# Second normalisation folded into centred weights, and a new hand-written order of jobs, in an attention and expert kernel on one core

## The reference, cut to what matters

```python
def layernorm(x):                       # no learned scale or shift
    return (x - mean(x)) / sqrt(var(x) + 1e-5)

n = layernorm(x)
Q, K, V, U = silu(n @ Wq), silu(n @ Wk), silu(n @ Wv), silu(n @ Wu)   # U is used as silu(U)
s = (Q @ K.T + bias[i - j]) / 4         # per head, causal, keys that are zero masked
x = x + (silu(s) @ V) * U

n = layernorm(x)
logits = n @ w_gate.T                   # 8 of them, the best two taken
g = softmax over the best two, else 0
x = x + sum_e g[e] * ((n @ w_in[e].T) @ w_out[e].T)
```

## Time and profile before

| | us |
|---|---|
| median of 3 runs | 286.77 |
| lowest, highest | 285.39, 286.88 |
| the profiled execution | 285.98 |
| its span, first to last instruction | 284.2 |
| PE busy in it | 263.2 |
| DVE busy | 230.0 |
| ACT busy | 225.0 |
| POOL busy | 146.6 |

### The profile page before, as it was taken

How to read it: one execution, slowest core, us unless ns; L and a number is a source line. 1 busy time by engine, 2 the same in 40 slices (tenths; PEclk the granted TensorE clock), 3 DMA queues, 4 the chain that set the end, 5 groups by cost and what they waited for, 6 DMA issues and landing times.

```text
span 284.2 us, 8464 instructions
## 1 busy us (share of the span) xinstructions
PE 263.2 (93%) x3146; PEld 124.3 (44%) x3146; DVE 230.0 (81%) x764; ACT 225.0 (79%) x434; POOL 146.6 (52%) x236
## 2 busy tenths in 40 slices
PE   7779799999999999999999998999987999999862
PEld 5435444355565434243354444433442544554420
DVE  6448453744689997989999986999999999896977
ACT  2667998998777899899998999897666977879600
POOL 6312235330104559645964494569765649548554
PEclk9979999999999999999999999999999999999998
DMA  4796216986950004991496027803890100100101
GB/s 115 172 305 194 75 17 193 208 180 211 235 131 22 2 2 133 236 190 21 147 229 164 3 78 231 175 6 79 221 232 26 35 4 3 37 2 2 38 3 37
DMA packets 27912, 31.24 MB, mean 110 GB/s; under 512 B 3032, under 2 KB 16856, under 8 KB 27872
## 3 DMA queue, kind: packets, MB, share of 16 engines
q1 hardware_dynamic: 24320, 28.28, 39.8%
...
...
## 4 chain that ended last, share of the span: by engine, by line
PE 69%; DVE 16%; ACT 4%; DMA 4%; issue 3%; SPq 1%; POOL 1%; DVEq 0%; ACTq 0%; POOLq 0%
PE jobp L648 23%; PE o_acc L639 20%; PE score L623 20%; DVE score L914 9%; DMA wout_s<-in_L_ffn_w_out 3%; PE jobp L677 2%; DVE ymix L1026 2%; ACT wts L784 2%; PE jobp L709 2%; ACT xn L797 1%; PE jobp L729 1%; DVE xs L1040 1%; DVE stats L953 1%; SPq L452 1%; PE o_acc L743 1%
## 5 line engine op out<-in xcount | busy, mean ns | idle before, releaser
L914 DVE TENSOR_TENSOR score<-score,bias_near 128x256 f32<-128x256 f32 (+3 forms) x288 | 113.2, 468 | 13.7 <-PE score L623 13.3
L782 ACT ACTIVATE wts<-score 128x512 f32<-128x512 f32 (+1 forms) x172 | 96.7, 592 | 20.5 <-DVE score L914 16.5
L565 POOL TENSOR_TENSOR ymix<-ymix 128x512 f32<-128x512 f32 (+2 forms) x90 | 74.6, 829 | 48.6 <-DVE ymix L1026 43.9
L784 ACT ACTIVATE wts<-score,far 128x512 f32<-128x512 f32 x120 | 73.8, 700 | 6.6 <-DVE score L914 5.3
L639 PE MATMUL o_acc<-wts,v_pad 128*32 128x512 f32 (+3 forms) x864 | 77.1, 458 | 0.7 <-ACT wts L782 0.7
L648 PE MATMUL jobp<-mm_e,xn2T 128*32 128x512 f32 x480 | 60.3, 593 | 0.3 <-ACT mm_e L854 0.3
L623 PE MATMUL score<-q_stack,k_stack 64*128 64x256 f32 (+3 forms) x336 | 47.9, 356 | 0.1
L1026 DVE TENSOR_TENSOR ymix<-jobp,gates 128x512 f32<-128x512 f32 x60 | 40.3, 685 | 6.4 <-PE jobp L648 5.9
L623 PEld LDWEIGHTS score<-q_stack,k_stack 64*128 64x128 f32 x336 | 30.4, 184 | 31.0 <-issue 28.5
L639 PEld LDWEIGHTS o_acc<-wts,v_pad 128*32 128x32 f32 x864 | 20.8, 108 | 29.8 <-issue 16.1
L623 PE MATMUL score<-xn2T,xs 32*128 32x512 f32 (+3 forms) x192 | 26.9, 520 | 0.7 <-ACT wts L782 0.7
...
## 6 DMA issues: line engine op xcount, KB each, us to landing
...
```

What stands on the lines that cost most here:

```text
L565: then_wait(pool.tensor_tensor(y[:, 0:n], y[:, 0:n], y[:, n:2 * n], ALU.add))
L782: act.activation(weights, score[bank][:, 0:n], ACT.Silu, scale=HD ** -0.5).then_inc(weighed[bank], 1)
L784: act.activation(weights, score[bank][:, 0:n], ACT.Silu, bias=far[:, h:h + 1], scale=HD ** -0.5)\
L914: ins = dve.tensor_tensor(score[bank][:, c + near:c + n], score[bank][:, c + near:c + n], bias, ALU.add)
```

## The change

The second normalisation is no longer computed as such. Its mean is taken out of the weights: a matrix `centre` (1 - 1/128 on the diagonal, -1/128 elsewhere) is multiplied into the expert matrices and into w_gate by a new job `CM`. Its rstd is multiplied into the gap and the gates of every unit, as before in the last one alone. So `norm2`, `xn2` and `centred` go, `T2` transposes `xs` itself after `SEL`, and POOL makes no shift for these. POOL's `scale` waits for the gates of the unit that used the same rstd before, and `best` waits for `scaled` in every unit.

In the last unit `T2` stands ahead of `SEL`: products with the identity lay the old rows out by features in its bank, and after the gate two more add `oT`. `BEFORE`, `BESIDE` and `AFTER` are new throughout. The diff is cut to its core:

```diff
 BEFORE = [
-    [("stats1", 0, 0), ("RB",), ("norm1", 0, 0), ("stats1", 0, 1), ("T1", 0, 0), ("Q", 0, 0), ("K", 0, 0),
-     ("norm1", 0, 1), ("V", 0, 0), ("MASK", 0, 0)],
+    [("stats1", 0, 0), ("RB",), ("T1", 0, 0), ("norm1", 0, 0), ("norm1", 0, 1), ("stats1", 0, 1), ("Q", 0, 0),
+     ("K", 0, 0), ("T1", 0, 1), ("V", 0, 0), ("K", 0, 1), ("Q", 0, 1), ("MASK", 0, 0), ("REL",)],
 ]
 BESIDE = [
-    [("T1", 0, 1), ("U", 0, 0), ("stats1", 1, 0), ("WT", 0)],
-    [("M", 0), ("stats1", 1, 1), ("WT", 1)],
-    [("Q", 0, 1), ("K", 0, 1), ("norm1", 1, 0), ("M", 1), ("V", 0, 1), ("T1", 1, 0), ("norm1", 1, 1)],
+    [("stats1", 1, 0), ("WT", 0)],
+    [("M", 0), ("WT", 1), ("stats1", 1, 1)],
+    [("CM", 2), ("U", 0, 0), ("norm1", 1, 0), ("M", 1), ("U", 0, 1), ("T1", 1, 0), ("norm1", 1, 1)],
...
+    [("CM", 1), ("MASK", 1, 1)],
...
+    [("FF", 0, 3, 1), ("LOG", 1), ("best", 1, 0), ("best", 1, 1), ("gates", 1)],
+    [("V", 2, 0), ("U", 1, 1), ("T2", 2), ("T1", 2, 1), ("FF", 0, 4, 0), ("tanh", 1), ("FF", 0, 4, 1)],
...
+    [("FF", 2, 7, 0), ("best", 6, 0), ("best", 6, 1), ("gates", 6)],
+    [("tanh", 6), ("FF", 2, 7, 1)],
...
-    [("FF", 3, 3, 1), ("T2", 7)],
-    [("LOG", 7), ("tanh", 7), ("best", 7, 0), ("best", 7, 1), ("gates", 7)],
+    [("FF", 3, 1, 1), ("FF", 3, 2, 0), ("best", 7, 0), ("LOG", 7)],
+    [("FF", 3, 2, 1), ("tanh", 7)],
+    [("FF", 3, 3, 0), ("best", 7, 1), ("FF", 3, 3, 1)],
+    [("gates", 7)],
     [("FF", 3, 4, 0), ("FF", 3, 4, 1)],
 ]
 AFTER = [
...
-    [("SEL", 8), ("stats2", 8), ("norm2", 8), ("FF", 3, 5, 0), ("T2", 8), ("LOG", 8), ("best", 8, 0),
-     ("best", 8, 1), ("gates", 8), ("FF", 3, 5, 1), ("FF", 3, 6, 0), ("FF", 3, 7, 0), ("FF", 3, 6, 1),
-     ("FF", 3, 7, 1), ("tanh", 8), ("MIX",)],
+    [("FF", 3, 5, 0)],
...
+    [("T2", 8), ("SEL", 8), ("stats2", 8), ("LOG", 8), ("best", 8, 0), ("best", 8, 1), ("gates", 8),
+     ("FF", 3, 5, 1), ("FF", 3, 6, 0), ("MIX",), ("FF", 3, 7, 0)],
...
+    [("tanh", 8), ("FF", 3, 6, 1), ("FF", 3, 7, 1)],
@@ POOL, scale @@
+                elif b > 0 and ln:
+                    pool.wait_ge(gates_ready, 1 + unit_before(args[0]))
...
-                if (args, ln) in [((LAST,), 1), ((0, 0), 0)]:
+                if ln or args == (0, 0):
                     pool.tensor_tensor(rstd[:, ln, ts], rstd[:, ln, ts], mhalf[:, ts], ALU.pow).then_inc(scaled, 1)
                     return
...
+            then_wait(pool.memset(centre[:], -1.0 / D))
+            pool.affine_select(out=centre[:], in_=centre[:], compare_op=ALU.not_equal, fill=1.0 - 1.0 / D, base=0,
+                               pattern=[[-1, P]], channel_multiplier=1).then_inc(centre_set, 1)
@@ PE, T1 and T2 @@
+                        if job == ("T2", LAST):
+                            ins = pe.matmul(bank[:, cols], xs[:, b, t], ident[:], start=k == 0, stop=False)
+                        else:
+                            ins = pe.transpose(bank[:, cols], xn1[:, t] if kind == "T1" else xs[:, b, t], ident[:])
+                    if job == ("T2", LAST):
+                        pe.wait_ge(gated, LAST + 1)
+                        for k, t in enumerate(tiles):
+                            ins = pe.matmul(bank[:, k * P:(k + 1) * P], ident[:], oT[:, t * P:(t + 1) * P], start=False, stop=k + 1 == len(tiles))
@@ PE, the new job; LOG now waits for ("CM", 2) and uses wg_c, the first FF waits for ("CM", 0) and ("CM", 1) @@
+                elif kind == "CM":
+                    k = args[0]
+                    pe.wait_ge(centre_set, 1)
+                    if k < 2:
+                        for e in range(k * E // 2, (k + 1) * E // 2):
+                            wait_drained(pe, ("M", e))
+                        ins = quarters(bank[:], centre[:], mm_e[:, k * E // 2:(k + 1) * E // 2].rearrange("p e d -> p (e d)"))
+                    else:
+                        pe.wait_ge(wg_in, 16)
+                        ins = quarters(bank[:, 0:E], centre[:], wg_s[:])
@@ ACT copies CM's bank back to mm_e, or to wg_c; its norm2 goes @@
@@ DVE, take_best and mix_gates, now in every unit; its norm2 of the last unit goes @@
+                    dve.wait_ge(scaled, SCALES.index(((u,), 1)) + 1)
+                    then_wait(ins)
+                    dve.tensor_tensor(gap[:, ts], gap[:, ts], rstd[:, 1, ts], ALU.mult).then_inc(top_ready, 1)
...
+                then_wait(dve.tensor_tensor(pick[:, 0, ts], pick[:, 0, ts], rstd[:, 1, ts].unsqueeze(2).to_broadcast([P, n, E]),
+                                            ALU.mult))
```

More of the change, by code:

```diff
@@ L106 @@
 SPLIT = {s: n for n, s in enumerate(SPLITS)}
-BANKED = ("RB", "T1", "Q", "K", "V", "U", "MASK", "SEL", "T2", "LOG", "FF", "WT", "M")
+BANKED = ("RB", "T1", "Q", "K", "V", "U", "MASK", "SEL", "T2", "LOG", "FF", "WT", "M", "CM")
 LAST = len(UNITS) - 1
 LAST_TILES = range(NT - 2, NT)
+T2_FIRST = LAST
 def all_near(group):
@@ L155 @@
-    [("K", 1, 1), ("T2", 0), ("split", 1, 1)],
-    [("WT", 4), ("M", 3)],
-    [("LOG", 0), ("best", 0, 0), ("V", 1, 0), ("M", 4)],
-    [("WT", 5), ("tanh", 0)],
-    [("M", 5), ("WT", 6)],
-    [("MASK", 1, 0), ("best", 0, 1)],
-    [("gates", 0)],
-    [("WT", 7)],
-    [("stats1", 2, 0), ("MASK", 1, 1), ("M", 6)],
-    [("M", 7), ("V", 1, 1), ("FF", 0, 0, 0), ("norm1", 2, 0), ("FF", 0, 0, 1), ("SEL", 1)],
-    [("FF", 0, 1, 0), ("T1", 2, 0)],
-    [("FF", 0, 1, 1), ("stats2", 1), ("U", 1, 1)],
@@ L191 @@
-    [("gates", 3), ("K", 3, 1), ("MASK", 3, 0)],
-    [("best", 4, 0), ("LOG", 4), ("FF", 1, 4, 0)],
-    [("FF", 1, 4, 1), ("best", 4, 1), ("FF", 1, 5, 0)],
-    [("FF", 1, 5, 1), ("split", 3, 1), ("tanh", 4)],
-    [("gates", 4), ("FF", 1, 6, 0)],
-    [("FF", 1, 6, 1), ("FF", 1, 7, 0)],
-    [("FF", 1, 7, 1)],
-    [("FF", 2, 0, 0)],
-    [("FF", 2, 0, 1), ("FF", 2, 1, 0)],
-    [("FF", 2, 1, 1), ("V", 3, 1)],
-    [("FF", 2, 2, 0), ("stats2", 5), ("SEL", 5)],
-    [("norm2", 5), ("FF", 2, 2, 1), ("FF", 2, 3, 0), ("MASK", 3, 1)],
@@ new lines @@
+    [("V", 2, 0), ("U", 1, 1), ("T2", 2), ("T1", 2, 1), ("FF", 0, 4, 0), ("tanh", 1), ("FF", 0, 4, 1)],
+    [("FF", 0, 5, 0), ("FF", 0, 5, 1), ("MASK", 2, 0)],
+    [("FF", 0, 6, 0), ("K", 2, 1)],
+    [("best", 2, 0), ("LOG", 2), ("stats1", 3, 0), ("V", 2, 1), ("Q", 2, 1), ("best", 2, 1), ("stats1", 3, 1)],
+    [("tanh", 2), ("FF", 0, 6, 1), ("MASK", 2, 1), ("split", 2, 1)],
+    [("U", 2, 0), ("norm1", 3, 0), ("gates", 2), ("FF", 0, 7, 0)],
+    [("FF", 0, 7, 1), ("FF", 1, 0, 0)],
+    [("FF", 1, 0, 1)],
@@ new lines @@
+    [("U", 2, 1)],
+    [("FF", 1, 1, 0), ("norm1", 3, 1), ("FF", 1, 1, 1)],
+    [("T1", 3, 0), ("T1", 3, 1)],
+    [("K", 3, 0)],
+    [("FF", 1, 2, 0), ("SEL", 3)],
+    [("FF", 1, 2, 1), ("T2", 3)],
+    [("stats2", 3), ("FF", 1, 3, 0), ("U", 3, 0)],
+    [("LOG", 3), ("FF", 1, 3, 1)],
+    [("best", 3, 0), ("Q", 3, 0), ("SEL", 4)],
+    [("tanh", 3), ("best", 3, 1), ("gates", 3), ("split", 3, 0), ("T2", 4)],
+    [("stats2", 4), ("V", 3, 0)],
+    [("K", 3, 1), ("LOG", 4)],
+    [("FF", 1, 4, 0), ("FF", 1, 4, 1)],
@@ new lines @@
+    [("FF", 1, 5, 0), ("best", 4, 0), ("Q", 3, 1), ("best", 4, 1), ("split", 3, 1)],
+    [("FF", 1, 5, 1), ("tanh", 4), ("FF", 1, 6, 0)],
+    [("gates", 4), ("FF", 1, 6, 1), ("MASK", 3, 0)],
+    [("FF", 1, 7, 0), ("FF", 1, 7, 1)],
+    [("FF", 2, 0, 0), ("MASK", 3, 1)],
+    [("FF", 2, 0, 1)],
+    [("FF", 2, 1, 0), ("V", 3, 1)],
+    [("FF", 2, 1, 1)],
+    [("FF", 2, 2, 0), ("FF", 2, 2, 1)],
+    [("SEL", 5), ("FF", 2, 3, 0), ("stats2", 5)],
+    [("T2", 5)],
+    [("best", 5, 0), ("tanh", 5), ("LOG", 5), ("U", 3, 1), ("best", 5, 1), ("gates", 5)],
[4 rows of a table added]
```

117 lines of the change are left out of this document (43 added, 74 removed), and 30 rows, old and new, of the table BESIDE.

## The result

The changed kernel takes 284.65 us (median of 20 runs, 283.42 to 286.87), the kernel before beside it 287.06 us (20 runs). The ratio is 0.9929, 95% interval 0.9912 to 0.9947: 0.7% or 2.0 us faster. The medians as printed differ by 2.4 us because the ratio leaves out three of the 20 runs before, at 290.7 us and more, which fell in a slower state. The change goes in the forecast direction, lies inside the forecast range, and is half of the 3.9 us. The profiled execution took 283.42 us, with a span of 281.5.

A forecast was written before the change was run, and what follows sets the result against it. TensorE leads with VectorE and ScalarE close behind, and 18 us of PE's steps are stalls. The terms from start to last unit sum to -3.9 us, from the 286.77 us median to 282.9 us; range 278.6 to 286.8.

The forecast's parts named there:

- Steps 8 to 17: These steps take 1.5 us more PE work into steps 13 to 16, which stalled 2.4 us: minus 0.7 us.
- Steps 18 to 35: Here 2.5 us more PE work and 2.2 us more on VectorE, 1 us absorbed: plus 1.5 us.
- Steps 36 to 48: Here 0.8 us less PE work, and the 1.0 us stall of step 41 partly gone: minus 1.2 us.
- Steps 49 to 63: PE has 7 us of stall, VectorE barely 1; VectorE's load sets the stretch, much as before: minus 1.0 us.
- The last unit: At the end, earlier gate and T2 waiting for it alone bring gap times rstd 1.5 us forward; minus 1.1 us counted here.
- The start: T1, K and Q of half 1 go ahead of the first scores, under PE's wait for wout: minus 1.0 us.
- The fourth rival: Longer pauses before 13 us put PE at half clock through the first work: 285.2 us, chance 0.08.
- Part 1: Normalisation leaves ScalarE in units 0 to 7: about 13 us net, little on the path; T2 needs only SEL's sum.
- Part 3: Centring products CM 0, 1 and 2 add 2.0 us on PE; CM 2's wait for w_gate taken as 0.
- VectorE waiting for tanh in order: Rival: gates of units 1 and 6 stand before their tanh, up to 7.2 us of waits, 290.1 us, chance 0.12.
- The halved stalls: Rival: freed ScalarE and short chain cut stalls from 18 us to 9: minus 8, 278.8 us, chance 0.20.
- VectorE's load as the bound of the middle: Rival: the middle's gains are eaten, only start and last unit stay: 285.6 us, chance 0.15.

The follow-up runs named there:

- e7: Changed kernel without the centring products CM 0 and CM 1 and their ScalarE copies, CM 2 kept: 0.9941 of the kernel before.
- e8: Changed kernel with the casts of split and the logits copies moved from VectorE to ScalarE, unit 5's tanh behind LOG and U: 1.0148 of before.
- e9: Changed kernel with 30 dummy 128-column activations put back on ScalarE after stats2 of units 0 to 7: 1.0236 of before, 293.86 us.
- e2: The changed kernel's algebra run through the old lists, norm2 left out and CM set in where its inputs are first made: 1.0117 of before.
- e1: Changed kernel without the two rstd products of units 0 to 7 on VectorE, the last unit keeping its own: 0.9893 of before.
- e3: Changed kernel with unit 5's tanh moved behind LOG and the copy of U: 0.9935 of before.
- e4: Changed kernel with the last unit's T2 behind SEL, two transposes of summed rows instead of four products: 0.9903 of before.
- e6: The kernel before with only the start of the lists from the changed one, CM left out: 1.0028 of before.
- e5: New algebra in the old lists, as e2, but with the CM products moved to other places: 1.0137 of before.

## Why the forecast was right in sign and half in size

- **Steps 8 to 17 (-0.7): -0.52.** Right, and for the reason given: e7 shows that CM's work lies in waits.
- **Steps 18 to 35 (+1.5): +2.18.** Undersized by 0.7 us. The step that failed is "1 us absorbed" of 2.5: 0.3 were. The stalls counted in these steps were taken as room for any engine's work, and work put in comes out at the end: e8 and e9 lengthen this stage too, by 2.87 and 3.03 us. Work taken out did not shorten it: in e2 ScalarE has 3.1 us less in it (54.46 us busy for 57.54), for 60.87 us and 60.78.
- **Steps 36 to 48 (-1.2): -1.69.** Right; step 41, with its stall, went from 4.75 to 2.37 us, partly because it has less work in it.
- **Steps 49 to 63 (-1.0): -0.12.** This is the largest miss, and the step of the forecast that failed: "with the norm chain gone, DVE's load sets it, much as before", and yet a gain of 1.0 was booked. VectorE was busy 49.53 us of 51.16 and is busy 49.28 of 51.04, so there was next to nothing to gain by the forecast's own rule. The chain of the earlier trace rows ended at 218.16 us as a wait of ScalarE; e2, which takes it away and adds the rstd products, has 51.15 us for 51.16. The products cost 0.61 us of the stage in the new lists (e1), and two drains of experts fewer (16 for 18, at 683 ns) stand against them. If the products cost as much in the old lists, the chain's end alone was worth about as much there; no run has the one without the other.
- **Steps 64 to 71 (-0.4): +0.04.** The 0.38 us of the last weights were read as a wait for ScalarE's tanh. The same was tried in another unit (e3) and was worth nothing. For this unit it is argued, not shown.
- **The last unit (-1.1): -1.40**, better by 0.3, though two of its reasons were off: the gate came 0.43 us earlier, not 0.7 (0.95 after the product's start for 1.38), and e4 shows the products in one bank to be worth nothing. Their price was right: two products behind the gate took 0.61 us for the forecast 0.6. The Trainium skill (TensorE: Matmul & The Clock Gate, Terms) has the transposing mode "4× faster for FP32"; taken as against a product, as the forecast took it, that makes an estimate of 1.2 us for the two. The trace does not agree: a transpose took 0.16 to 0.20 us (four in 0.63, two in 0.39) and a product 0.31.
- **The start (-1.0): not shown.** The medians leave 0 to 1.0 us for it, e6 has no gain from the new start in the old kernel, and the two profiles, which differ by 1.19 us at step 8, can't tell: they differ by 3.4 us for the same kernel code. The fourth rival, "a slow TensorE at the start", was written as a case that holds or not. It holds in some executions of this kernel and not in others: of the ten profiled executions with all of the new start, four kept the full clock from 16 to 28 us. CM 2 did not wait for w_gate; step 1 takes 7.38 us with it and 7.32 without (e6).

In sum from step 8 on: forecast -2.9, measured -1.51. **Part 1** said of the ScalarE time saved (13 us, 9.1 on the page) that "little of it is on the path by itself" and that what counts is the shorter way to T2. e2, which has both of these and pays for the rstd products, gains 0.2 us from step 18 to 63, so both together are worth little more there than the products cost. What was missing is that the new order spends what was freed: put 12.4 us back there, and 8.1 come out at the end (e9). **Part 3** had 2.0 us more on PE: in the old order 3.7 to 4.1 us (e5, e2), with whatever else the algebra moved there, in the new one 0 to 0.4 us for 1.7 (e7). So the algebra in the old lists costs 1.2%, and from there the lists give 1.9%. Nobody ran the new lists with the old normalisation, so how much of the 1.9% the lists would give without the algebra is open; e9, which brings back ScalarE's load alone, loses more than that.

Of the rivals, VectorE waiting for tanh in order did not come: its waits list over the whole changed kernel has

```profile
DVE pick L1106 <- ACT half_tanh L866: 0.5, 1, 0.5
```

0.5 us where 7.2 was the price. The halved stalls did not come either. (Its own terms, 9 less, 1.4 more and 1.1 less, make 8.7 us, not 8.) VectorE's load as the bound of the middle is the rival that was nearest: it was right about steps 49 to 63 and wrong about 36 to 48. Of the marks set out to look for, ScalarE near 212 us (215.9), VectorE near 232 (233.2), the first product with v (22.35) and 5.7 us in the last unit (5.39) are met or nearly; the last product near 266 us (267.70) and steps 49 to 63 a microsecond shorter are not.

No version ran that beats the changed kernel with all of its work; e3 and e4 are as fast as it within their intervals.
